# Attention and experts on one core: the output projection tile by tile in the next chunk, and the value product in 64x64 pieces skewed over two units

## The chip, the cores and the metric

The kernel runs on one NeuronCore of a Trainium2 chip. The time is the device time of one execution in microseconds, the median of three runs. TensorE (PE in the rows) multiplies, VectorE (DVE), ScalarE (ACT) and GpSimd (POOL) work on elements, and SyncE (SP) issues DMAs. Each engine works through its own list in order; semaphores hold an instruction back until another engine has counted far enough.

## The reference

A transformer layer on 2x2048 tokens of 256 numbers: attention in a window of 128 keys over 16 heads of 64, and a mixture of 8 experts, top 2, with 640 slots per expert and choice.

```python
h = _layernorm(x) * (1 + ca) + sa
q, k, v = split(h @ Wqkv)                      # 16 heads of 64
scores = (q @ k.T) * scale                     # keys j with i-127 <= j <= i
attn = softmax(where(mask, scores, -max)) @ v
x = x + ga * (attn @ Wout)
h = _layernorm(x) * (1 + cb) + sb
probs = softmax(h @ gate_w.T + gate_b); topk_prob, topk_idx = top_k(probs, 2)
# each token goes to a slot of its two experts, in order of tokens, at most 640 per expert and choice
y = sum over choices of prob * (relu(xb @ W1 + b1) @ W2 + b2)
x = x + gb * y
```

## The kernel before

**Tiling.** The 4096 tokens are 8 chunks of 512 (`NC`), a chunk is 4 tiles of 128. The projections and the output use pairs of 16-bit numbers (high and low part, three products each); scores, transposes and the value product work on 32-bit numbers. A chunk has 16 *units*: a pair of heads `j` and one half (`part`) of the chunk, that is 4 tiles of 128 queries by 256 keys.

**Steps.** A chunk runs in 16 steps, `i` = 4 to 19 (`STEPS`). In step `i` TensorE makes the scores of unit `i` (from 16 on those of the next chunk's first four), the value product of unit `i-4`, the transposes of unit `i-2` and one projection of q or k for the next chunk, in steps 12, 13, 14 and 16 also one tile of the first half of the next chunk's values. VectorE masks, takes the row maxima, normalises the unit before, and at every second step forms the low part of the attention output; ScalarE does the exponentials of unit `i-1` (`exponentials`), the high part (`attn_high`), the copy of the turned probabilities out of PSUM (`copy_probT`) and the copies of the projections; GpSimd splits the turned probabilities into the part for the block before and the part for the own block (`split_keys`), zeroing what the mask forbids.

**Between chunks.** After step 19 TensorE makes the second half of the next chunk's values (`projections_after`, 4 tiles) and the output projection of the whole chunk (`project_out`, 96 matmuls of 256 columns), and VectorE adds it to `x` (`add_attention`).

**Routing.** The tokens of the chunk before are normalised, scaled, packed and sent to the experts' slots along the steps: `ROUTE_AT` says at which step each part stands. GpSimd does the scale and shift, and the scattering DMAs (`scatter`). In the last chunk the steps are others (`LAST_AT`, `EARLY_AT`), and the last projections (`LATE`) are made there.

**PSUM.** Two banks each for the two score buffers, one for the transposes (`pt`), one for the value product (`pv`), and two (`gen`) that all projections, logits, counts and outputs take in turn: `group_order` gives the n-th group bank n mod 2, and a group waits until the engine that empties the one before it in this bank has done so (`claim`). All orders are written out by hand; nothing is scheduled by a program.

The lines that the change touches most:

```python
for hd in range(2):                                  # L666, value product, two matmuls of 256 columns
    mm = pe.matmul(pv[r:r + DH, 2 * part * P:(2 * part + 2) * P], v[:, 2 * part + 1, h * DH:(h + 1) * DH], ...)
for i in range(2):                                   # L671, four of 128
    for hd in range(2):
        mm = pe.matmul(pv[r:r + DH, b * P:(b + 1) * P], v[:, b + i, h * DH:(h + 1) * DH], ...)
```

## Time and profile before

| | us |
|---|---|
| three timed runs, median (lowest, highest) | 1151.61 (1149.98, 1154.63) |
| profiled execution, its own time | 1147.24 |
| its span | 1144.4 |
| chunk 0, steps and what follows (54.4 to 135.4) | 81.0, TensorE busy 79.7 |
| chunk 1 (135.4 to 218.7) | 83.3, TensorE busy 81.6 |
| chunk 6 (551.8 to 625.6) | 73.8, TensorE busy 68.9 |
| last chunk and way into the experts (625.6 to 760) | 134.4, TensorE busy 110.6 |
| experts (760 to the end) | 384.4, TensorE busy 373.0 |

Over the span TensorE is busy 95%, VectorE 66%, ScalarE 58%, GpSimd 44%. The granted clock of TensorE is full (1.00) in all attention chunks but the last (0.95). A time in a row is counted from the start of the span. The last column of a timeline row, in brackets, is the idle time of the engine ahead of the row and what ended it.

### The profile page before, as it was taken

To read this page: it belongs to the slowest core of one execution; us is meant where nothing else is said; L and a number is where in the kernel's file an instruction comes from. 1 tells how busy PE (TensorE), PEld (TensorE's weight loads), DVE (VectorE), ACT (ScalarE), POOL (GpSimd) and SP (SyncE) were. 2 spreads that over 40 slices of the span, in tenths; PEclk is the share of its full clock that TensorE was granted. 3 is DMA by queue.
4 is the path that set the end of the run, shared out by engine and by line. 5 is a ranking of instruction groups with operands and counts; after the bars stand their busy time and mean duration, and the time that the engine had idled before them with its cause. 6 is when DMAs were issued, how large, how long until landed. Compare 5 with 4: busy or idle time off the path is not lost.

```text
span 1144.4 us, 25293 instructions
## 1 busy us (share of the span) xinstructions
PE 1084.4 (95%) x9469; PEld 711.8 (62%) x9469; DVE 750.3 (66%) x1663; ACT 660.5 (58%) x1874; POOL 506.2 (44%) x555
## 2 busy tenths in 40 slices
PE   7999999999999999999998885989999999999996
PEld 4455655655655655655656564756776858585765
DVE  5776586586576585674675784756676766666653
ACT  5677476476476476476473853447474563727461
POOL 2234274365275365355445655434344352525342
PEclk9999999999999999999999998999999999999998
DMA  9744111112021021021031024434345353534000
GB/s 335 151 163 138 40 29 48 38 37 52 27 45 48 24 46 45 24 45 39 24 103 48 5 83 121 92 94 81 109 94 153 97 112 111 112 112 78 23 20 9
DMA packets 140114, 87.41 MB, mean 76 GB/s; under 512 B 96708, under 2 KB 130650, under 8 KB 139868
## 3 DMA queue, kind: packets, MB, share of 16 engines
q1 hardware_dynamic: 129244, 64.29, 21.4%
q0 software_dynamic: 10752, 21.54, 6.6%
q8 instruction: 75, 1.23, 0.5%
q14 instruction: 43, 0.35, 0.1%
HBM read 40.02 MB, written 33.79 MB: 64 GB/s over the span
## 4 chain that ended last, share of the span: by engine, by line
PE 75%; issue 7%; DVE 7%; ACT 6%; POOL 4%; DMA 0%; SPq 0%; POOLq 0%; DVEq 0%; ACTq 0%
PE down L1617 18%; PE up L1603 17%; PE gen L600 10%; PE gen L614 7%; PE gen L691 6%; PE score L637 4%; PE pv L668 4%; PE pt L648 4%; ACT prob L909 4%; PE pv L675 3%; DVE prob L1121 2%; POOL h L370 1%; POOL probT_split L1424 1%; PE gen L699 1%; POOL probT_split L1422 1%
## 5 line engine op out<-in xcount | busy, mean ns | idle before, releaser
L1643 ACT ACTIVATE hid<-up,b1T 128x512 f16<-128x512 f32 (+2 forms) x192 | 124.3, 648 | 182.1 <-PE up L1603 180.3
L1603 PE MATMUL up<-xT,w 128*128 128x512 f16 (+2 forms) x1152 | 212.5, 346 | 10.9 <-issue 10.9
L1617 PE MATMUL down<-w,hid 128*128 128x256 f16 x1920 | 213.7, 274 | 3.2 <-DVE hid L1659 3.2
L1422 POOL TENSOR_SCALAR_AFFINE_SELECT probT_split<-probT 128x512 f32<-128x512 f32 x128 | 102.9, 804 | 250.9 <-ACT probT L917 247.4
L1617 PEld LDWEIGHTS down<-w,hid 128*128 128x128 f16 x1920 | 188.6, 98 | 27.6 <-DVE hid L1659 3.7
L600 PE MATMUL gen<-hT,big 128*128 128x512 f16 x768 | 185.0, 380 | 0.6 <-DVE hT L1371 0.6
L909 ACT ACTIVATE prob<-score,negmax 128x128 f32<-128x128 f32 x512 | 180.7, 375 | 0.7 <-DVE negmax L1113 0.7
L1603 PEld LDWEIGHTS up<-xT,w 128*128 128x128 f16 x1152 | 112.9, 98 | 104.9 <-issue 12.8
...
L1659 DVE TENSOR_TENSOR hid<-hid 128x512 f16<-128x512 f32 (+2 forms) x192 | 115.2, 606 | 72.4 <-ACT hid L1644 72.0
L917 ACT ACTIVATE probT<-pt 128x512 f32<-128x512 f32 x128 | 76.9, 601 | 99.0 <-PE pt L648 98.8
L1109 DVE COPY_PREDICATED score<-above,score 128x512 f32<-128x512 int32 x112 | 77.5, 692 | 77.3 <-PE score L637 77.2
L1644 ACT ACTIVATE hid<-up,b1T 128x512 f32<-128x512 f32 (+2 forms) x192 | 124.8, 650 | 0.0
L600 PEld LDWEIGHTS gen<-hT,big 128*128 128x128 f16 x768 | 73.8, 98 | 67.7 <-issue 1.2
L637 PE MATMUL score<-k,q 64*64 64x192 f32 (+2 forms) x2048 | 111.0, 330 | 2.6 <-issue 2.2
L909 ACT ACTIVATION_READ_ACCUMULATOR prob<-score,negmax 128x1 f32 x512 | 111.0, 217 | 0.0
...
L1121 DVE TENSOR_TENSOR prob<-prob,rinv 128x512 f32<-128x512 f32 x128 | 103.4, 808 | 0.0
L668 PE MATMUL pv<-probT_split,v 128*64 128x256 f32 x512 | 83.5, 403 | 19.0 <-DVE attn L1134 7.0
L637 PEld LDWEIGHTS score<-k,q 64*64 64x64 f32 x2048 | 64.5, 132 | 53.9 <-issue 51.6
L614 PE MATMUL gen<-big,hT 128*128 128x512 f16 x384 | 89.1, 379 | 2.3 <-DVE logit L1160 1.2
L1424 POOL TENSOR_SCALAR_AFFINE_SELECT probT_split<-probT 128x512 f32<-128x512 f32 x128 | 86.3, 674 | 0.0
...
## 6 DMA issues: line engine op xcount, KB each, us to landing
...
kept<-out,tail POOLq DMA_INDIRECT x80, 3.1
out<-y,tail POOLq DMA_INDIRECT x80, 2.4
...
```

Source lines behind the costliest of these rows:

```text
L600: mm = pe.matmul(dst[:], wqkv[:, kd, a, col:col + P], hT[:, cn % 2, kd, b, :], start=(n == 0), stop=(n == 5))
L614: mm = pe.matmul(dst[:], hT[:, cn % 2, kd, a, s * P:(s + 1) * P], wqkv[:, kd, b, 2 * INNER + half * 512:2 * INNER + (half + 1) * 512], sta ...
L637: mm = pe.matmul(dst[lo:lo + HALF, 2 * hd + i, first:lo + P + HALF], q[r:r + DH, j, b * P + lo:b * P + lo + HALF], k[r:r + DH, j, b * P + ...
L668: mm = pe.matmul(pv[r:r + DH, 2 * part * P:(2 * part + 2) * P], v[:, 2 * part + 1, h * DH:(h + 1) * DH], probT_split[:, par, 2 * hd:2 * hd ...
L909: mm = act.activation(prob[:, h % 2, b, :], score[h % 2][:, b, P:], ACT.Exp, bias=negmax[:, h % 2, b:b + 1], accum_out=rowsum[:, h % 2, b: ...
L1121: dve.tensor_tensor(prob[:, h % 2], prob[:, h % 2], rinv[:, h % 2, :].unsqueeze(2).to_broadcast([P, TILES, P]), ALU.mult)\
L1422: pool.affine_select(out=probT_split[:, h % 2, :, 1], in_=probT[:, h % 2], pattern=[[0, TILES], [1, P]], compare_op=ALU.is_ge, fill=zero, ...
L1603: mm = pe.matmul(bank, w1[:, par, kd, a, ft * P:(ft + 1) * P], part_rows(e, n, xT[:, par, b * KD + kd, :]), start=(i == 0), stop=(i == 5))
L1617: mm = pe.matmul(down[n][:, s, :], hid[:, ft, a, t * P:(t + 1) * P], w2[:, par, ft, b, :], start=(i == 0), stop=(i == 3 * FT - 1))
L1643: act.activation(part_rows(e, n, hid[:, ft, 0, :]), bank, ACT.Relu, scale=1 / W_SCALE, bias=bias).then_inc(hid_hi, 1)
L1644: act.activation(part_bank(e, n, hid32[:, k_ % 4, :]), bank, ACT.Relu, scale=1 / W_SCALE, bias=bias).then_inc(up_out, 1)
L1659: dve.tensor_tensor(part_rows(e, n, hid[:, ft, 1, :]), part_bank(e, n, hid32[:, k_ % 4, :]), part_rows(e, n, hid[:, ft, 0, :]), ALU.subtra ...
```

## The change

- The output projection of chunk c is made tile by tile in steps 4, 6, 8 and 11 of chunk c+1 (`OUT_TILE`, `late_out`, `add_tile`), and the second half of the values of a chunk in its own steps 5, 7, 9 and 10 (`SECOND_V`). Chunk 6 makes its output at its own end as before, in pairs of tiles (`project_out_pair`).
- The value product of chunks 0 to 6 is cut into 64x64 pieces: `high_keys` takes keys 64 to 127 of a block, `low_keys` keys 0 to 63; pieces that the mask empties are left out. In step `i` the high keys of unit `i-4` stand in turn with the low keys of unit `i-5` (`half_values`), also over the border of two chunks. There are two banks `pv` now, one per parity of the unit.
- The transposes take the two `gen` banks like everything else (`("pt", i)`); their own bank is gone. ScalarE copies them straight to `probT_split`, which is a ring of three, and GpSimd splits in place.
- Routing is spread over two chunks: rows in steps 8 to 16 (`ROUTE_AT`), logits to scatter in steps 4 to 13 of the next (`CHOOSE_AT`); for round 6 they stand at the end of chunk 6.
- The high and low parts of the attention output are made per unit (256 columns) in a ring of 24 slots (`attn_slot`). `x` holds 6 chunks instead of 8 (`X_PLACE`), the last two are loaded late. The weights of expert 0 are loaded after chunk 6's rows are stored.

```diff
+X_PLACE = (2, 3, 0, 1, 4, 5, 2, 3)
+X_CHUNKS = max(X_PLACE) + 1
+ATTN_SLOTS = H + PAIRS
+LATE_PACKED = (ATTN_SLOTS - H) * 4 * P
 EARLY_TILES = 3
+RING = 3
...
 score = [ps(f"score{i}", [P, TILES, 2 * P], F32) for i in range(2)]
-pt = ps("pt", [P, TILES, P], F32)
-pv = ps("pv", [P, CHUNK], F32)
+pv = [ps(f"pv{i}", [P, CHUNK], F32) for i in range(2)]
 gen = [ps(f"gen{i}", [P, 512], F32) for i in range(2)]
...
+OUT_TILE = {4: 0, 6: 1, 8: 2, 11: 3}
+SECOND_V = {5: 0, 7: 1, 9: 2, 10: 3}
+ROUTE_AT = {"stats": (8, 13), "rstd": 13, "norm": 14, "scale": 14, "shift": 15, "token": 16, "pack": 16, "low": 16}
+CHOOSE_AT = {"logits": 4, "softmax": 5, "exp": 5, "top": 6, "counts": 7, "slots": 8, "send": 9, "sent": 13}
...
+        names += [("pt", i)]
+        if c > 1:
+            names += ([("logits",)] if i == CHOOSE_AT["logits"] else []) + ([("counts",)] if i == CHOOSE_AT["counts"] else [])
         if c > 0:
...
+            names += [("tile", OUT_TILE[i])] if i in OUT_TILE else []
+            names += [("own v", SECOND_V[i])] if i in SECOND_V else []
+        names += projections_at(c, i)
...
+        def high_keys(c, u, hd, i, cur):
+            n_unit = H * c + u
+            j, part = unit_of(c, u)
+            r, h, b = DH * hd, 2 * j + hd, 2 * part + i
+            first = HALF * cur
+            return pe.matmul(pv[n_unit % 2][r:r + DH, i * P + first:(i + 1) * P], v[HALF:, b + cur, h * DH:(h + 1) * DH],
+                             probT_split[HALF:, n_unit % RING, 2 * hd + i, cur, first:], start=(i == 0 and cur == 0),
+                             stop=False, skip_group_check=True)
+        def low_keys(c, u, hd, i, cur):
+            n_unit = H * c + u
+            j, part = unit_of(c, u)
+            r, h, b = DH * hd, 2 * j + hd, 2 * part + i
+            last = P if cur else HALF
+            return pe.matmul(pv[n_unit % 2][r:r + DH, i * P:i * P + last], v[0:HALF, b + cur, h * DH:(h + 1) * DH],
+                             probT_split[0:HALF, n_unit % RING, 2 * hd + i, cur, 0:last], start=False,
+                             stop=(cur == 0), skip_group_check=True)
+        def half_values(c, new, old):
+            if old is not None:
+                pe.wait_ge(high_done, H * old[0] + old[1] + 1)
+            if new is not None:
+                values_there(c, new)
+            for i in range(2):
+                for n in range(2):
+                    for hd in range(2):
+                        if new is not None:
+                            high = high_keys(c, new, hd, i, n)
+                        if old is not None:
+                            low = low_keys(*old, 1 - hd, i, 1 - n)
+            if new is not None:
+                high.then_inc(high_done, 1)
+            if old is not None:
+                low.then_inc(pv_done, 1)
...
+        def late_out(c, t):
+            if c == 0 and t == 0:
+                pe.wait_ge(split_lo, 8)
+            pe.wait_ge(attn_lo, H * c + (H - 1 if t < 2 else H))
+            dst, full = claim(c + 1, ("tile", t))
+            project_out_tile(c, dst[:, 0:D], t, range(PAIRS)).then_inc(full, 1)
...
+                if c == LAST - 1 and i == STEPS[-1]:
+                    half_values(c, i - HI_AT, (c, i - LO_AT))
                     scores(c, i)
-                weighted_values(c, i - 4)
...
+                    half_values(c, None, (c, H - 1))
+                else:
+                    scores(c, i)
+                    half_values(c, i - HI_AT, (c, i - LO_AT) if i >= LO_AT else (c - 1, H - 1) if c > 0 else None)
+                transposes(H * c + i - 2, c, ("pt", i))
+                if c > 1 and i == CHOOSE_AT["logits"]:
+                    route_logits(c - 1)
+                if c > 1 and i == CHOOSE_AT["counts"]:
+                    route_counts(c - 1)
+                if c > 0 and i in OUT_TILE:
+                    late_out(c - 1, OUT_TILE[i])
+                if c > 0 and i in SECOND_V:
+                    project_v(c - 1, 1, [SECOND_V[i]])
+                for name in projections_at(c, i):
+                    project(c, name)
+            if c == LAST - 1:
...
-            act.activation(probT[:, h % 2], pt[:], ACT.Copy).then_inc(probT_ready, 1)
...
+            bank, before = turned_in(u)
+            act.wait_ge(gen_full[bank], before + 1)
+            at_least(act, pv_done, u - RING + 1)
+            act.activation(probT_split[:, u % RING, :, 1], gen[bank][:].rearrange("p (a q) -> p a q", q=P), ACT.Copy)\
+               .then_inc(gen_free[bank], 1)
         def attn_high_part(c, u):
             j, part = unit_of(c, u)
...
             act.wait_ge(pv_done, H * c + u + 1)
...
+            if c > 0 and u == ATTN_SLOTS - H:
+                bank, before = group(c - 1, ("out", 1)) if c == LAST else group(c, ("tile", TILES - 1))
+                act.wait_ge(gen_full[bank], before + 1)
+            act.activation(attn[:, attn_slot(c, j, part), 0, :], pv[(H * c + u) % 2][:, 0:2 * P], ACT.Copy).then_inc(attn_hi, 1)
...
+                exponentials(c, i - 1)
+                if i >= LO_AT:
+                    attn_high_part(c, i - LO_AT)
+                elif c > 0:
+                    attn_high_part(c - 1, H - 1)
+                if c > 1 and i == CHOOSE_AT["exp"]:
+                    route_exp(c - 1)
+                if c > 0 and i == at["pack"]:
                     route_pack(c)
                 if i == LN_AT[1] + 1 and c + 2 < NC:
                     ln_pack(c + 2)
...
+                copy_probT(c, i - 2)
+                if c > 0 and i in SECOND_V:
+                    values(c - 1, ("v", 1, SECOND_V[i]))
+                for name in projections_at(c, i):
+                    evacuate(c, name)
+            if c == LAST - 1:
+                attn_high_part(c, H - 1)
                 for name in projections_after(c):
                     evacuate(c, name)
...
+                route_exp(c)
...
+        def add_tile(c, t):
+            bank, before = group(c + 1, ("tile", t))
+            if c == 0 and t == 0:
+                dve.wait_ge(mod_spread, 16)
+            at_least(dve, x2_ready, TILES * c + t)
+            dve.wait_ge(gen_full[bank], before + 1)
+            dve.scalar_tensor_tensor(gated[:, t % 2, :], gen[bank][:, 0:D], 1 / W_SCALE, modrow[:, batch(c), 0, :],
+                                     ALU.mult, ALU.mult).then_inc(gen_free[bank], 1)
+            dve.wait_ge(gen_free[bank], before + 1)
+            row = x[:, x_at(c) + t, :]
+            dve.tensor_tensor(row, row, gated[:, t % 2, :], ALU.add).then_inc(x2_ready, 1)
...
+                if i > LO_AT:
+                    attn_low_part(c, i - LO_AT - 1)
+                elif c > 0:
+                    attn_low_part(c - 1, H + i - LO_AT - 1)
+                if c > 0 and i == LO_AT:
+                    keep_v(c - 1, 1)
+                if c > 0 and i - 1 in OUT_TILE:
+                    add_tile(c - 1, OUT_TILE[i - 1])
+                if c > 1 and i == CHOOSE_AT["softmax"]:
+                    route_softmax(c - 1)
+                if c > 1 and i == CHOOSE_AT["slots"]:
+                    route_slots(c - 1)
+                if c == 0 and i % 2 == 0:
+                    keep_first_keys((i - LAG) // 2)
+                if i == 13:
+                    keep_v(c, 0)
+                softmax_step(c, i, False)
+                if c > 0 and i in at["stats"]:
+                    half = at["stats"].index(i)
+                    dve.wait_ge(x2_ready, TILES * (c - 1) + 2 * half + 2)
+                    norm_stats(dve, x_at(c - 1), stats[1], meanvar[1], r_stat, r_mv, stats_before(c) + half + 1,
+                               range(2 * half, 2 * half + 2))
+                if c > 0 and i == at["norm"]:
+                    norm_rows(dve, x_at(c - 1), h2, meanvar[1], rstd[1], r_rstd, r_xn, c)
+                if c > 0 and i == at["token"]:
+                    route_tokens(c)
+                if c > 1 and i == CHOOSE_AT["top"]:
+                    route_top(c - 1)
+                if i in LN_AT and c + 2 < NC:
+                    ln_shift(c + 2, LN_AT.index(i))
+                if i == LN_NEXT and c + 3 < NC:
+                    ln_first(c + 3)
+                if i == LN_NEXT + 1 and c + 3 < NC:
+                    ln_second(c + 3)
+            if c == LAST - 1:
+                for u in range(H - 2, H):
+                    attn_low_part(c, u)
+                keep_v(c, 1)
+                route_softmax(c)
+                route_top(c)
+                add_attention(c, 0)
+                route_slots(c)
+                add_attention(c, 1)
...
-            pool.affine_select(out=probT_split[:, h % 2, :, 1], in_=probT[:, h % 2], pattern=[[0, TILES], [1, P]],
+            bank, before = turned_in(u)
+            pool.wait_ge(gen_free[bank], before + 1)
+            whole, own = probT_split[:, u % RING, :, 1], probT_split[:, u % RING, :, 0]
+            pool.affine_select(out=own, in_=whole, pattern=[[0, TILES], [-1, P]],
+                               compare_op=ALU.is_gt, fill=zero, base=0, channel_multiplier=1).then_inc(prev_ready, 1)
+            pool.affine_select(out=whole, in_=whole, pattern=[[0, TILES], [1, P]],
                                compare_op=ALU.is_ge, fill=zero, base=0, channel_multiplier=-1).then_inc(cur_ready, 1)
-            pool.affine_select(out=probT_split[:, h % 2, :, 0], in_=probT[:, h % 2], pattern=[[0, TILES], [-1, P]],
...
+                if c > 1 and pick["send"] <= i < pick["send"] + TILES:
+                    scatter(c - 1, [i - pick["send"]])
+                if c > 1 and i == pick["sent"]:
+                    pool.wait_ge(sent, 16 * TILES * K * (c - 1))
+                if i == LN_NEXT + 1 and c + 3 < NC:
+                    ln_rstd_of(c + 3)
+            if c == 0:
+                pool.wait_ge(zero_sent, 16 * (SLOTS // P))
+            if c == LAST - 1:
+                scatter(c, range(TILES))
+                pool.wait_ge(sent, 16 * TILES * K * c)
```

**TensorE in a step with nothing but scores, values, transposes and a projection, before** (L637 scores, L668 and L675 value product, L648 transposes, L600 a projection of k; `pv` and `gen` are PSUM banks):

```order
L637 MATMUL score1<-k,q 64x192 x8
L668 MATMUL pv<-probT_split,v 64x256 x2
L675 MATMUL pv<-probT_split,v 64x128 x4
L648 MATMUL pt<-identf,prob 128x128 x4
L600 MATMUL gen1<-hT,big 128x512 x6
```

**The same engine after, first step of chunk 3** (L716 high keys of the new unit, L725 low keys of the old one; L686 scores, L696 transposes; below the first half of the pieces, the second is the same again):

```order
L686 MATMUL score0<-k,q 64x192 x8
L716 MATMUL pv0<-probT_split,v 64x128
L725 MATMUL pv1<-probT_split,v 64x128
L716 MATMUL pv0<-probT_split,v 64x128
L725 MATMUL pv1<-probT_split,v 64x128
L716 MATMUL pv0<-probT_split,v 64x64
L725 MATMUL pv1<-probT_split,v 64x64
L716 MATMUL pv0<-probT_split,v 64x64
L725 MATMUL pv1<-probT_split,v 64x64
...
L696 MATMUL gen0<-identf,prob 128x128 x4
L826 MATMUL gen1<-gate16,h2T 128x8 x24
L768 MATMUL gen0<-wout,attn 128x256 x24
```

The six value matmuls of one unit have become sixteen, eight of them of the unit before, in the other bank. The logits (L826) and output tile 0 (L768) stand behind the transposes, and tile 0 takes the bank that the transposes have just filled.

**TensorE between two chunks before** (L614 values, second half; L691 output projection):

```order
L600 MATMUL gen1<-hT,big 128x512 x6
L614 MATMUL gen0<-big,hT 128x512 x6
L614 MATMUL gen1<-big,hT 128x512 x6
L614 MATMUL gen0<-big,hT 128x512 x6
L614 MATMUL gen1<-big,hT 128x512 x6
L691 MATMUL gen0<-wout,attn 128x256 x48
L691 MATMUL gen1<-wout,attn 128x256 x48
L637 MATMUL score0<-k,q 64x192 x8
```

This block is gone but for chunk 6; its parts stand as the tiles of L768 and L663 in the steps of the next chunk.

**VectorE ahead of step 5 of a chunk, after** (L1368 low part, L1211 the values' last tile kept for the next chunk, L1264 and L1268 addition of output tile 0, L1282 the logits read out of PSUM, L1222 the mask of step 5):

```order
L1234 TENSOR_TENSOR prob<-prob,rinv 128x512
L1368 TENSOR_TENSOR attn<-pv1,attn 128x256
L1211 COPY v<-v 128x512
L1264 SCALAR_TENSOR_TENSOR gated<-gen0,modrow 128x256
L1268 TENSOR_TENSOR x<-x,gated 128x256
L1282 SCALAR_TENSOR_TENSOR logit<-gen1,gbB 128x32
L1222 COPY_PREDICATED score1<-above,score1 128x4x128
```

The addition and the logits were at the chunk's end and in step 13; now the reading of the logits, which empties gen1, stands behind the addition of tile 0. The low part follows each normalisation (L1234) instead of every second.

**ScalarE in step 16, after** (L1045 packing of the routed rows, L1024 copy of the turned probabilities, L998 q, L1005 values):

```order
L1015 ACTIVATE prob,rowsum<-score1,negmax 128x128 x4
L1033 ACTIVATE attn<-pv1 128x256
L1045 ACTIVATE packed<-h2 128x4x256
L1024 ACTIVATE probT_split<-gen0 128x4x128
L998 ACTIVATE q<-gen1 128x512
L1005 ACTIVATE v<-gen0 128x512
```

The packing was in step 9, two steps behind the shift; it is now one step behind it, ahead of the copy that empties gen0 for the value tile.

## Rows read from the trace of the kernel before

**Rows 1.** Busy time by stretch, chunk 3; columns as in the first row.
```profile
core 0: us, PE busy (x) PEld busy (x) DVE busy (x) ACT busy (x) POOL busy (x), PEclk, DMA share, GB/s
...
302.10:385.20 83.10, 81.44 (x795) 50.04 (x794) 56.37 (x139) 51.36 (x179) 41.79 (x48) 1.00 0.15 40
```

**Rows 2.** Timeline of TensorE, one step of chunk 3: start, duration, line, tiles, count.
```profile
305.77 0.88 PE L637 MATMUL score<-k,q 64*64 64x192 f32 x16
306.58 0.65 PE L668 MATMUL pv<-probT_split,v 128*64 128x256 f32 x4
307.06 0.61 PE L675 MATMUL pv<-probT_split,v 128*64 128x128 f32 x8
307.60 0.66 PE L648 MATMUL pt<-identf,prob 128*128 128x128 f32 x4
308.10 1.46 PE L600 MATMUL gen<-hT,big 128*128 128x512 f16 x6
309.49 0.88 PE L637 MATMUL score<-k,q 64*64 64x192 f32 x16
```

**Rows 3.** Timeline of TensorE, between chunks 3 and 4.
```profile
369.40 5.34 PE L614 MATMUL gen<-big,hT 128*128 128x512 f16 x24
374.58 10.64 PE L691 MATMUL gen<-wout,attn 128*128 128x256 f16 x96
```

**Rows 4.** Timeline of TensorE, chunk 3, steps 8 and 12.
```profile
316.91 0.88 PE L637 MATMUL score<-k,q 64*64 64x192 f32 x16
318.38 0.65 PE L668 MATMUL pv<-probT_split,v 128*64 128x256 f32 x4 [0.59 <-POOL probT_split L1424]
...
335.24 0.75 PE L740 MATMUL gen<-gate,h2T 128*128 128x8 f16 x24
...
337.51 1.47 PE L614 MATMUL gen<-big,hT 128*128 128x512 f16 x6 [0.21 <-DVE logit L1160]
```

**Rows 5.** Timeline of TensorE, windows of 0.1 and 0.7 us at two scores.
```profile
302.06 0.39 PE L637 MATMUL score<-k,q 64*64 64x192 f32 x4
...
353.56 0.77 PE L637 MATMUL score<-k,q 64*64 64x64 f32 x16
354.27 0.44 PE L668 MATMUL pv<-probT_split,v 128*64 128x256 f32 x2
```

**Rows 6.** Timeline of ScalarE, the step of rows 2.
```profile
306.37 0.36 ACT L909 ACTIVATE prob<-score,negmax 128x128 f32<-128x128 f32 x1
...
307.74 0.62 ACT L923 ACTIVATE attn<-pv 128x512 f16<-128x512 f32 x1
308.30 0.60 ACT L917 ACTIVATE probT<-pt 128x512 f32<-128x512 f32 x1
```

**Rows 7.** Timeline of VectorE, the step of rows 2, and step 10.
```profile
308.57 0.68 DVE L1121 TENSOR_TENSOR prob<-prob,rinv 128x512 f32<-128x512 f32 x1
309.17 0.69 DVE L1134 TENSOR_TENSOR attn<-pv,attn 128x512 f16<-128x512 f32 x1
...
328.09 1.11 DVE L1121 TENSOR_TENSOR prob<-prob,rinv 128x512 f32<-128x512 f32 x1
```

**Rows 8.** Timeline of GpSimd, chunk 3.
```profile
314.35 2.36 POOL L370 TENSOR_TENSOR h<-h,modrow 128x1024 f32<-128x1024 f32 x1 [4.01 <-DVE h L237]
...
328.03 0.63 POOL L1424 TENSOR_SCALAR_AFFINE_SELECT probT_split<-probT 128x512 f32<-128x512 f32 x1
```

**Rows 9.** Timeline of TensorE, chunk 6, step 14 and after step 19.
```profile
593.06 0.88 PE L637 MATMUL score<-k,q 64*64 64x192 f32 x16
...
612.38 2.75 PE L614 MATMUL gen<-big,hT 128*128 128x512 f16 x12
```

**Rows 10.** Timeline of GpSimd, scattering DMAs at the end of chunk 6.
```profile
602.59 1.11 POOL L1433 DMA_INDIRECT slot_inputs<-packed,send  x1 [1.98 <-DVE send L1227]
604.00 0.98 POOL L1433 DMA_INDIRECT slot_inputs<-packed,send  x1 [0.30 <-PE pv L675]
...
618.73 0.63 POOL L1422 TENSOR_SCALAR_AFFINE_SELECT probT_split<-probT 128x512 f32<-128x512 f32 x1 [1.61 <-DMA slot_inputs<-packed,send]
```

**Rows 11.** Timeline of SyncE's queue, the four transposes for chunk 2.
```profile
111.80 6.17 SPq L535 DMA_TRANSPOSE hT<-h  x4
```

561 lines of the change are left out of this document (268 added, 293 removed).

## Prediction

> **What bounds the kernel now.** I read the busy time by stage first: the table above and, for one full chunk, [rows 1]. One full round of the attention (a chunk of 512 tokens, 16 head units) takes 83.1 us of which TensorE is busy 81.4, at the full granted clock; VectorE is busy 56, ScalarE 51, GpSimd 42. So a chunk costs what TensorE has to do plus its few waits. By the table chunk 0 takes 81.0, chunks 1 to 5 83.3 each, chunk 6 73.8, the last chunk and the way into the experts 134, the experts 384. The change touches the first 626 us and the last chunk.
>
> The timeline of TensorE in a step without extras [rows 2] gives scores 306.58-305.77 = 0.81, value product 307.60-306.58 = 1.02, transposes 0.50, one q or k projection 1.39: 3.72 us, and the next step follows at once. Between two chunks stand 24 matmuls of values (5.2 us) and 96 of the output projection (10.6 us) [rows 3]: TensorE is busy all through, so there is no hole to fill there. TensorE's waits inside a chunk are small. Taking each step's scores-to-values distance against 0.81, and the 0.36 before a value projection, they are 0.66, 0.25, 0.26, 0.36 and 0.57, together 2.1 us; the first and the fourth are in [rows 4], on GpSimd's split of the turned probabilities and on VectorE's logits. The others are on the split and on VectorE's low half of the attention output.
>
> **The value product.** Before, a unit has 2 matmuls of 256 columns and 4 of 128; each column half of the array gets 256+2x128 = 512 columns. Now each quarter of the array gets 2x128+2x64 = 384, because 64x64 blocks that the mask empties are left out, and the upper keys of one unit run beside the lower keys of the unit before. What a column costs follows from [rows 2]: scores put 2x192 = 384 columns through the busiest quarter in 0.81, values 512 in 1.02. Two equations: 1.64 ns a column and 0.18 us fixed for going from one kind of product to the next. The first unit of a batch checks it: 128+192 = 320 columns in the busiest quarter, 0.18+0.52 = 0.70, measured 354.27-353.56 = 0.71 [rows 5].
>
> Now scores and values are both of the 64x64 kind, so I count the fixed part once: 0.18+768x1.64 = 1.44 against 0.81+1.02 = 1.83. That is a gain of 0.39 at most; the pieces per quarter rise from 4 to 8, for which I keep back 0.03 and take **0.36 us a step**. The low bound is the fixed part paid twice: 0.36-0.18 = 0.18. Both are estimates from [rows 2, 5]. Chunks 0 to 6 have 112 such steps. In the last six of chunk 6 TensorE doesn't set the pace (below): 106x0.36 = **-38.2 us**.
>
> How close small matmuls can follow: 24 of 8 columns over the whole array take 0.61 us, 25 ns each [rows 4], while four passes of scores, each in another quarter, cover 0.39 us together [rows 5]; one after another, at 192x0.82 ns each, they would cover over 0.63. The Trainium skill (TensorE: Matmul & The Clock Gate, "Wait — 56ns, not 53.3ns?") says that start-to-start never drops below about 25 ns however small a matmul is. By it the 32 passes of a unit's values would need 0.80 us instead of 0.63. The logits agree; the scores' row speaks against such a floor across quarters, and no run here shows 32 in a row. The same skill (TensorEngine Tiling (Array Packing), "Key Properties") says that changing the tiling mode drains the array; the 0.18 fixed agrees in kind, and by that rule it is paid once.
>
> **Output projection and second half of the values.** The same 96+24 matmuls, moved into steps 4 to 11 of the next chunk: 0 us of work. Chunk 6 keeps its own output at its end. On VectorE two additions of 512 columns (0.69 each op) become four of 256; the low half of the attention goes from 8x512 to 16x256, and it is now wanted in every step. VectorE has 27 us of slack a chunk, so only the places count. The old waits go with the old places: 2.1 in each of chunks 1 to 5 and about 1.5 in chunk 6: **-12.0 us**.
>
> **What is late next.** The transposes lose their own bank and share the two gen banks, in turn. Times below are from a step's start. A copy of the turned probabilities now ends at about 2.95: exponentials run 0.59 to 1.97, the high half of 256 columns takes some 0.35 (an estimate from 0.56 for 512), the copy 0.6 [rows 6].
>
> a) Step 4, chunks 2 to 6: transposes gen0, logits gen1, tile 0 gen0, q0 gen1. Tile 0 is reached at 2.58 and waits for the copy, 0.4. It ends at 5.6. VectorE stands at the addition of tile 0, and the logits behind it are what frees gen1 for q0: about 0.2 to hear of it, two additions of 0.35, 0.18 for the logits: 6.8 instead of 5.6. Together 1.6.
> b) Step 7, chunks 2 to 6: counts take gen1, so the value tile needs gen0 at 2.3 and waits until 2.95; k1 then meets VectorE's route_slots within 0.1. Together 0.75.
> c) Steps 10 and 11: normalising rows of 0.88 to 1.6 delay the low half, which TensorE wants 0.70 into a step: 0.2.
> d) Steps 15 and 16: GpSimd has scale and shift of 2.36 each [rows 8] two steps apart, fed by VectorE's 1.6 us of rows at step 14. Scale ends 2.85 into step 15, so the split behind it reaches TensorE 0.25 late; VectorE's low half adds 0.2. Shift ends 3.25 into step 16; ScalarE's packing (1.05) stands in step 16 ahead of the copy, which ends at 5.0 instead of 2.95, and the value tile in gen0 was due at 3.66: 1.35. Together 1.8.
> e) Step 18: statistics and rows of chunk c+3 (1.8+1.7) now lie in steps 16 and 17: 0.5.
>
> Sum 4.85 a chunk in chunks 2 to 5: 19.4. Chunk 1 has only c to e, 2.5, and one thing more: the 80 zero rows hold SP until 111.8, then four transposes end at 118.0 plus their landing [rows 11]; chunk 0 now ends near 113.4 and q0 wants them at 118.0: 1.5. Chunk 6, first ten steps: 2.5. **+25.9 us.** The bounds of this term are wide: some of these waits lie under each other, 0 at the lowest; twice as much if VectorE's extras meet GpSimd's (its normalise takes 0.68 alone and 1.11 when a split has begun before it [rows 7, 8]).
>
> Chunk 6, steps 14 to 19, have no q and k. Before they took 612.38-593.06 = 19.3 for 14 us of work [rows 9]. Now scale, shift and low stand in exactly these steps: 5.2 until the rows are there, scale, split, shift, split, packing, low, two splits, 2.36+1.4+2.36+1.4+0.1+2.4+3x1.45: about 20.6 with the value tile (1.3) that moved in. **0 us.**
>
> Into the last chunk: round 6's scatter, 8 DMAs, is now one block after its slots. Logits come 3.4 after step 19, the first output pair at 8.7, two additions and the slots at 12.2. The pairs of DMAs cost 1.11+0.30+0.98 [rows 10], so 9.5 for eight, and 1.6 for the landing [rows 10]: 23.3. TensorE is there at 14.1+5.8+0.8 = 20.7 and needs one split, 0.8 to 1.5, more: 3.5 to 4. The last chunk has waits on GpSimd of its own later and takes part of it back: **+2.5 us.** The weights of expert 0 load later, but 7.8 us ahead of their use in step 7.
>
> **Sum**: -38.2-12.0+25.9+0+2.5 = -21.8 us. The profiled execution took 1147.2 (span 1144.4), so 1125.4; the median of the three timed runs lies 4.4 above it. Forecast 1129, a little under 1129.8.
>
> **Rivals.**
> R1, the small pieces cost more: the fixed part is paid twice (0.18), or each of the 32 passes holds TensorE for 25 ns as the logits' matmuls do, 32x0.025 = 0.80 instead of 384x1.64 = 0.63 (0.17). 106x0.17 = 18 us of the gain are gone: 1147. For it: every other change of product in [rows 2] costs this; against: between the two kinds of value matmuls nothing extra stands. The floor named by TensorE: Matmul & The Clock Gate in the Trainium skill would act in this way.
> R2, slower than before: VectorE's low half decides each step. The place is TensorE's value product at step i, which wants the low half of unit i-6; VectorE does that one right after normalising [rows 7]. Normalise starts 2.8 into a step, ends at 3.4, low half 0.4 more: 3.85, wanted at 3.36+0.70 = 4.06. The margin is 0.2. If the copy of the turned probabilities is ready before 2.8, GpSimd's split goes first and normalise takes 1.11: TensorE then waits about 0.45 in all 106 steps, +48 us: 1177. It decides from a delay of 0.2 on; by my count the split begins at 2.98, 0.17 after normalise (starts of both from [rows 6, 7], less the shorter high half).
> R3, the waits a to e mostly cover each other, half of 25.9: 1116.
>
> **Numbers.** Forecast 0.60, R1 0.20, R2 0.10, R3 0.10. A difference under 0.5% (5.8 us) can't be told from none. Faster by more: forecast, R3, and somewhat under half of R1, 0.78; within 0.5%: the rest of R1, 0.11; slower 0.11. Range 1112 (under R3) to 1151 (over R1); the 0.10 of R2 stays out.
>
> **What would show it.** Quiet steps of TensorE of 3.36 instead of 3.72, and scores to transposes 1.47 instead of 1.83 (R1: 1.65). Chunks 2 to 5 at 80.4, chunk 0 at 59. Waits of q0 on VectorE's logits in step 4, of tile 0 and step 7's and step 16's value tile on ScalarE's copy. A wait of TensorE on VectorE's low half in nearly every step would be R2. In chunk 6 the last six steps unchanged near 20, and one wait on GpSimd of 3 to 4 us at the second unit of the last chunk. I am wrong if a full chunk still takes over 83.

## The result, and the profile after

The changed kernel takes 1157.61 us (median of 7 runs, 1155.87 to 1160.58) where the kernel before takes 1151.61 (7 runs, 1149.69 to 1154.63): 1.0053 times as long, 95% interval 1.0038 to 1.0068. Forecast were 1129, and 1151 as the upper end of the range. The profiled execution took 1158.6, its span 1155.9.

The experiments ran in five groups. Kernels of one group ran one after the other on one chip, with runs of the kernel before among them (medians 1151.8, 1149.4, 1150.6, 1153.4, 1148.0). In three further measurements the changed kernel took 1.0048 (1.0035 to 1.0062), 1.0067 (1.0040 to 1.0093) and 0.9991 (0.9975 to 1.0006) of it: it is a little slower, or the same, and never the 2% faster that was forecast.

What was promised of the value product is there. A quiet step of the changed kernel (chunk 3, against [rows 2]; the columns are start, busy us, engine, line, operation):

```profile
325.39 0.88 PE L686 MATMUL score<-k,q 64*64 64x192 f32 x16
326.09 0.27 PE L725 MATMUL pv<-probT_split,v 64*64 64x128 f32 x1
...
326.87 0.66 PE L696 MATMUL gen<-identf,prob 128*128 128x128 f32 x4
327.36 1.46 PE L649 MATMUL gen<-hT,big 128*128 128x512 f16 x6
328.75 0.88 PE L686 MATMUL score<-k,q 64*64 64x192 f32 x16
```

328.75-325.39 = 3.36 us instead of 3.72, and 326.87-325.39 = 1.48 from scores to transposes (forecast 1.47). But TensorE is no longer busy all through. The first block shows one full chunk (chunk 4) and the last chunk, with the columns of [rows 1]; the second what TensorE waits for up to the last chunk (what ends the wait, then us in total, times, longest):

```profile
363.90:446.50 82.60, 77.75 (x1111) 51.93 (x1110) 58.38 (x156) 51.77 (x187) 43.88 (x49) 1.00 0.16 40
...
621.50:714.90 93.40, 64.85 (x677) 42.41 (x676) 59.60 (x164) 45.39 (x148) 51.11 (x58) 0.93 0.27 81
```

```profile
PE pv L716 <- DVE attn L1368: 8.5, 9, 2.2
PE gen L663 <- ACT probT_split L1024: 7.5, 12, 0.9
PE gen L649 <- DVE logit L1282: 6.2, 5, 1.2
PE pv L716 <- POOL probT_split L1565: 5.8, 8, 1.7
PE gen L696 <- issue: 1.8, 7, 0.3
PE gen L768 <- issue: 1.2, 4, 0.3
```

A full chunk still takes 82.6, of which TensorE is busy 77.8; in [rows 1] it was 81.4 of 83.1. The busy time went down by 3.7 and the idle time up by 3.2. (In the profile without pauses, of which more below, chunk 4 takes 80.5, with 76.5 busy.) Here is where each profiled execution left the forecast's sum (1125.4 us of execution, 1122.6 of span). The column of the forecast is the time of before with the terms of its own sum (for a full chunk they give 80.3; its text says 80.4); the second profile is that of the fifth group.

| stretch, us | before | forecast | after, first profile | after, fifth group |
|---|---|---|---|---|
| up to chunk 0 | 54.4 | 54.4 | 55.0 | 55.8 |
| chunk 0 | 81.0 | 59.4 | 62.3 | 62.3 |
| chunk 1 | 83.3 | 79.4 | 77.5 | 77.5 |
| chunks 2, 3, 4, 5 | 83.3, 83.1, 83.4, 83.3 | 80.3 each | 82.7, 86.5, 82.7, 82.5 | 80.8, 83.6, 80.5, 79.8 |
| chunk 6 | 73.8 | 87.0 | 92.4 | 90.6 |
| last chunk to the first expert product | 81.8 | 84.3 | 93.4 | 100.0 |
| from there to the end | 437.0 | 437.0 | 441.0 | 437.7 |

The first profile is 33.2 us over the sum. Of these 11.5 are pauses in chunks 2 to 6 that came in some groups and not in others (the two profiles' chunks differ by that), 9.1 the last chunk, and 8.1 what both profiles share in chunks 0 to 6: chunks 0, 3 and 6 are 2.9, 3.3 and 3.6 over, chunk 1 is 1.9 under. The 4.0 us in the experts are in the first profile alone (the other three of this kernel give 437.7 to 438.5); their cause stays open. In the fifth group's profile the last chunk alone is 15.7 over.

### The profile page after: what moved, and what is told of

Read it like the earlier page. It is cut to its first block, busy times and chain, and to the rows that moved or that the text cites. A ratio compares the mean times of both kernels' runs of the same rounds, so it can differ in the third digit from the quotient of the medians.

```text
span 1155.9 us, 29944 instructions
## 1 busy us (share of the span) xinstructions
PE 1065.9 (92%) x11709; PEld 728.6 (63%) x11709; DVE 764.2 (66%) x1743; ACT 664.2 (57%) x1930; POOL 516.0 (45%) x555
## 4 chain that ended last, share of the span: by engine, by line
PE 75%; DVE 7%; ACT 6%; issue 6%; POOL 4%; DMA 1%; SPq 0%; DVEq 0%; ACTq 0%; another core or an unknown queue 0%; POOLq 0%
PE down L1773 17%; PE up L1759 17%; PE gen L649 12%; PE gen L768 7%; PE gen L663 6%; PE score L686 5%; PE gen L696 4%; ACT prob L1015 3%; PE pv L725 3%; PE pv L716 2%; DVE prob L1234 1%; POOL h L404 1%; POOL h L408 1%; ACT probT_split L1024 1%; DVE xn L1185 1%
## 5 line engine op out<-in xcount | busy, mean ns | idle before, releaser
L1563 POOL TENSOR_SCALAR_AFFINE_SELECT probT_split<-probT_split 128x512 f32<-128x512 f32 x128 | 110.2, 861 | 260.4 <-ACT probT_split L1024 255.7
L649 PE MATMUL gen<-hT,big 128*128 128x512 f16 x768 | 187.8, 384 | 11.5 <-DVE logit L1282 6.2
L1858 POOL DMA_INDIRECT out<-y,tail x80 | 82.5, 1031 | 209.9 <-DVE y L1843 195.9
L1222 DVE COPY_PREDICATED score<-above,score 128x512 f32<-128x512 int32 x112 | 77.7, 694 | 98.9 <-PE score L686 98.6
L686 PE MATMUL score<-k,q 64*64 64x192 f32 (+2 forms) x2048 | 111.0, 330 | 2.2 <-issue 2.2
L716 PE MATMUL pv<-probT_split,v 64*64 64x64 f32 (+1 forms) x1792 | 97.0, 245 | 14.6 <-DVE attn L1368 8.5
L716 PEld LDWEIGHTS pv<-probT_split,v 64*64 64x64 f32 x1792 | 92.4, 133 | 25.0 <-issue 23.9
L663 PE MATMUL gen<-big,hT 128*128 128x512 f16 x384 | 92.6, 380 | 9.1 <-ACT probT_split L1024 7.5
L725 PE MATMUL pv<-probT_split,v 64*64 64x128 f32 (+1 forms) x1792 | 99.9, 246 | 0.2
L686 PEld LDWEIGHTS score<-k,q 64*64 64x64 f32 x2048 | 64.5, 132 | 55.4 <-issue 52.7
L725 PEld LDWEIGHTS pv<-probT_split,v 64*64 64x64 f32 x1792 | 93.8, 133 | 1.8 <-issue 0.2
```

Of the source, the lines that this page charges most:

```text
L649: mm = pe.matmul(dst[:], wqkv[:, kd, a, col:col + P], hT[:, cn % 2, kd, b, :], start=(n == 0), stop=(n == 5))
L663: mm = pe.matmul(dst[:], hT[:, cn % 2, kd, a, s * P:(s + 1) * P], wqkv[:, kd, b, 2 * INNER + half * 512:2 * INNER + (half + 1) * 512], sta ...
L686: mm = pe.matmul(dst[lo:lo + HALF, 2 * hd + i, first:lo + P + HALF], q[r:r + DH, j, b * P + lo:b * P + lo + HALF], k[r:r + DH, j, b * P + ...
L716: return pe.matmul(pv[n_unit % 2][r:r + DH, i * P + first:(i + 1) * P], v[HALF:, b + cur, h * DH:(h + 1) * DH], probT_split[HALF:, n_unit ...
L725: return pe.matmul(pv[n_unit % 2][r:r + DH, i * P:i * P + last], v[0:HALF, b + cur, h * DH:(h + 1) * DH], probT_split[0:HALF, n_unit % RIN ...
L1563: pool.affine_select(out=own, in_=whole, pattern=[[0, TILES], [-1, P]], compare_op=ALU.is_gt, fill=zero, base=0, channel_multiplier=1).the ...
```

## The experiments

**The value product, undone.** Chunks 0 to 6 use the old product in the new arrangement:

```diff
-    half_values(c, i - HI_AT, (c, i - LO_AT) if i >= LO_AT else (c - 1, H - 1) if c > 0 else None)
+    weighted_values(c, i - HI_AT)
```

> The changed kernel with one part undone: chunks 0 to 6 use the value product of before (2 matmuls of 256 columns and 4 of 128 per unit, all keys of one unit together) in the new arrangement of output projection, values and routing. Forecast's term: 0.36 us in each of 106 steps where TensorE sets the pace, 38 us: 1196. If steps that wait for VectorE, ScalarE or GpSimd hide part of it, the chunks 2 to 5 lose less than 5.8 us each: with four or five waiting steps a chunk, 4.0 to 4.8, and about 1185 to 1190.

Measured: 1172.47 (first group). The chunks 0 to 6 take 578.3 together against 555.0 for the changed kernel in its profile without pauses (the fifth group's): the new product is worth 23.3 us there, not 38.2. Step by step the difference is 0.35 where TensorE sets the pace. But step 16 is 5.49 with the old and 6.19 with the new product, step 18 4.20 and 4.37: there TensorE waits for something that stands at its own time, and shorter steps before only make the wait longer. Another 1.3 is step 17 of chunk 3 (7.23 and 8.54), where TensorE's granted clock fell in the one profile and not in the other; more on it below. It was run again beside the changed kernel:

> The old value product in the new arrangement once more, against the changed kernel on the same chip. Worth of the new product by the step lengths of the two profiles so far: 0.35 in each quiet step, less where a step waits for something else; 3.4 to 4 a chunk, about 24 to 27 in all: the time is that much above the changed kernel's. If TensorE's pauses come from its many instructions (32 small matmuls a unit instead of 6, 40% more instructions in all), this kernel has none on the chip that shows them, and the difference is only 15 to 18 there.

> The changed kernel once more, as the partner on one chip of the three that follow. So far one chip showed TensorE pausing with nothing to wait for while the scatter's packets are out (steps 9 to 13 of chunks 2 to 6, 2 us a chunk), another chip did not, in other variants. If it is the chip: either this run has the pauses and the three others have them too where they issue as many TensorE instructions, or none has. 1153 to 1158 with them, 1145 to 1149 without.

Measured in the third group: 1172.16 against 1156.93, so the new product was worth only 15.2 there. The reason is in the next rows.

**The pauses.** In the first profile, in steps 9 to 13 of chunks 2 to 6, TensorE stops between two instructions with nothing to wait for that the profile shows; its granted clock is 1.00 there. Step 10 of chunk 3, first profile:

```profile
314.67 0.33 PE L696 MATMUL gen<-identf,prob 128*128 128x128 f32 x1
315.17 0.42 PE L696 MATMUL gen<-identf,prob 128*128 128x128 f32 x2 [0.17 <-issue]
315.91 0.27 PE L696 MATMUL gen<-identf,prob 128*128 128x128 f32 x1 [0.32 <-issue]
316.01 1.46 PE L663 MATMUL gen<-big,hT 128*128 128x512 f16 x6
```

and the same step of the same program in the fifth group:

```profile
313.43 0.66 PE L696 MATMUL gen<-identf,prob 128*128 128x128 f32 x4
313.92 1.46 PE L663 MATMUL gen<-big,hT 128*128 128x512 f16 x6
```

Four transposes cover 1.51 us instead of 0.66. GpSimd issues the scatter's DMAs in steps 9 to 12; outside steps 9 to 13 no step of these chunks differs between the two profiles by more than 0.2. Steps 9 to 13 of chunk 3 take 26.1 instead of 23.5.

> The changed kernel itself, run once more beside the others. In its first profile VectorE's first instruction of a step (the mask of the new scores) starts 0.3 to 0.8 us after everything it needs, in the four steps 9 to 12 of chunks 2 to 6 in which GpSimd issues the scatter's DMAs, and steps 9 to 13 together take 24.5 to 26.2 us; in the three variants of it run so far it starts after 0.07, and these steps take 23.5. Theory 1 (the stalls belong to this program, whatever chip runs it): they are back, chunks 2 to 5 take 82.5 and more, and the time is 1155 to 1160. Theory 2 (they belonged to that one placement on a chip): chunks 2 to 5 at 80.8, the experts at 437 instead of 441, and 1142 to 1148.

Measured: 1154.42, and the pauses were back in all four kernels of this second group (the changed kernel's chunks 2 to 5 took 82.5, 84.2, 82.5, 81.7). The three variants of the first group had none. In the third group the changed kernel, `spread_again` and `best1` had them, and `whole_again`, with 6 matmuls a unit instead of 32, had not: its steps 9 to 13 take 25.1 in both groups. So the scatter alone doesn't make them; this one comparison speaks for the many small instructions as a second condition (TensorE and its loads issue 10955 instructions from 200 to 600 us, in the kernel before 7855). I then put the old product into these steps only:

```diff
+    elif c > 1 and 9 <= i <= 14:
+        scores(c, i)
+        if i == 9:
+            half_values(c, None, (c, i - LO_AT))
+        if i < 14:
+            weighted_values(c, i - HI_AT)
+        else:
+            half_values(c, i - HI_AT, None)
```

> The changed kernel with the old value product (6 matmuls a unit instead of 32) in steps 9 to 13 of chunks 2 to 6 only, where the scatter's DMAs go out, and the new one elsewhere; at step 9 TensorE does the low keys of the unit before apart, at step 14 the high keys alone. Instruction theory (TensorE pauses there because its instructions are too many for what it is fed while the scatter's packets are out): VectorE's mask follows the scores after 0.07 in all these steps; by lengths they take 5 x 0.35 more work but 2.0 to 2.6 less of pauses, so the time is within 3 us of the changed kernel's. Rival (the pauses come from the scatter alone): they stay, and the time is 8 us longer, 1163 to 1165.

Measured: 1155.46, in the fourth group, in which no kernel paused; so it tells nothing of the pauses. (Step 9 takes 5.67 instead of 4.66, since the low keys of one unit stand alone.)

> The changed kernel a fourth time. Three chips were met in the calls so far: on one, every kernel with the new value product paused in the scatter's steps, on two, none did, and the four edits together took 1137.3 on the first and 1125.8 on another. If that holds for the change alone, it takes 1154 to 1157 where its profile shows the pauses (chunks 2 to 5 at 82 to 85) and 1143 to 1148 where it does not (chunk 2 at 80.8), which would be below the kernel before.

Measured: 1147.39, the kernel before 1147.96. This was the same chip as in the second and third group, and there was no pause. The time that the expectation gave for a run without pauses (1143 to 1148) holds, but its reason, the chip, does not: neither the chip nor the program decides alone, and within a group all went the same way. What it is stays open. The Trainium skill (Runtime: NRT & Kernel Launch, "Instruction fetch mechanics") says that an engine's instructions are fetched in blocks of 16 KiB, 256 instructions each, by a DMA queue of their own. The trace agrees on the size (42 fetches, 672 KB, for these 10955 instructions), but not on a cause: the fetches next to the pause above begin at 309.4 and 320.5.

**The last chunk: block of scatter DMAs and weights of expert 0.** The change puts the eight DMAs of round 6 in one block ahead of the last chunk's second split, and behind them asks for 2 MB of weights. The weights moved back into chunk 6 (they go to other places in the memory for that, the old ones being still in use, and ScalarE's splits of them get one more wait):

```diff
-store_rows(LAST - 1)
 sp.wait_ge(kept_clean, 1)
 sp.wait_ge(x2_sent, 16 * (LAST - 1))
+sp.wait_ge(r_xn, LAST - 1)
 load_expert(sp, weights_32(0), 0)
+store_rows(LAST - 1)
```

> The changed kernel with one thing moved back: the 2 MB of expert 0's weights are asked for near the end of chunk 6's steps, ahead of the store of chunk 6's rows, into the places of x that chunks 4 and 5 have left, and no longer at the start of the last chunk. Theory (collision): in the changed kernel this transfer fills the DMA engines just when ScalarE, TensorE and GpSimd enter the last chunk's code; the second step of that chunk takes 11.9 us instead of 5.8, ScalarE's first high half there starts 4.5 us after its data, and the landing of the scatter takes 4.7 us instead of 1.6. With the transfer gone from there the second step should be 7 to 9 us, and the whole 4 to 8 us shorter: 1150 to 1154. Rival (the block of eight scatter DMAs on GpSimd alone makes the step long): the step stays at 10 us or more and the time within 2 us of 1157.6.

Measured: 1141.85, 0.9927 (0.9898 to 0.9956) of the kernel before. The 15.8 us to the first measurement are not all this edit's, since its group had no pauses. Against the fifth group, without pauses too but on another chip, it is 5.5 in the medians and 9.2 in the last chunk of the profiles (90.8 for 100.0). TensorE and GpSimd at the second unit of the last chunk, with the weights early:

```profile
617.97 0.97 POOL L1575 DMA_INDIRECT slot_inputs<-packed,send  x1 [0.30 <-issue]
...
620.57 0.63 POOL L1564 TENSOR_SCALAR_AFFINE_SELECT probT_split<-probT_split 128x512 f32<-128x512 f32 x1 [1.62 <-DMA slot_inputs<-packed,send]
...
621.88 1.12 PE L755 MATMUL pv<-probT_split,v 128*64 128x256 f32 x4 [4.00 <-POOL probT_split L1564]
```

and in the changed kernel (fifth group), with TensorE's granted clock of this stretch (the column behind GpSimd's, then the DMA share and GB/s):

```profile
618.19 0.97 POOL L1574 DMA_INDIRECT slot_inputs<-packed,send  x1 [0.30 <-issue]
...
624.07 0.63 POOL L1563 TENSOR_SCALAR_AFFINE_SELECT probT_split<-probT_split 128x512 f32<-128x512 f32 x1 [4.91 <-DMA slot_inputs<-packed,send]
...
625.39 1.12 PE L754 MATMUL pv<-probT_split,v 128*64 128x256 f32 x4 [7.82 <-POOL probT_split L1563]
...
628.21 4.12 PE L649 MATMUL gen<-hT,big 128*128 128x512 f16 x12
```

```profile
616.00:622.00 6.00, 0.88 (x16) 0.56 (x16) 2.52 (x9) 1.99 (x9) 2.56 (x3) 0.89 1.00 347
622.00:628.00 6.00, 2.60 (x16) 1.98 (x17) 0.18 (x1) 0.38 (x1) 3.65 (x6) 0.50 0.23 85
628.00:634.00 6.00, 5.27 (x32) 2.29 (x33) 1.90 (x5) 2.83 (x10) 3.60 (x3) 0.75 0.00 0
```

With the weights early the scatter lands after 1.62, as in [rows 10], and TensorE waits 4.00: the forecast's 3.5 to 4. With the weights behind it the landing takes 4.91, because the DMA engines are full (share 1.00, 347 GB/s), and TensorE waits 7.82. Its granted clock falls from 2.4 to 1.2 GHz during the wait in both kernels, and it stays low for longer behind the longer one: here it is 0.50 from 622 to 630 us (in the middle row above) and 1.00 again from 632; with the weights early it is 0.50 for some 3 us:

```profile
621.80:624.00 2.20, 2.12 (x13) 1.50 (x14) 0.00 (x0) 0.10 (x1) 2.12 (x4) 0.50 0.00 0
```

So q and k take 4.12 here and 2.81 with the weights early, and this step 16.4 and 11.2, instead of 5.8. The expectation had 7 to 9, the rival 10 or more with nothing gained in time: both were half right. In the groups with pauses the loss lies in two steps (11.9 and 6.9 in the first profile). The two steps together are 18.8 to 22.2 in all nine profiles with late weights and a block, 17.1 with early weights and a block, 11.6 in that of before. To see whether the transfer harms by itself, the kernel before got it at the same place (`load_expert` behind the last `store`, splits in steps 7 to 10):

> The kernel before with the same transfer moved the other way: expert 0's weights are asked for at the start of the last chunk instead of during chunk 6, and their splits stand two steps later (steps 7 to 10), as in the changed kernel. The scatter, the value product and all the rest are those of before. Collision theory: the first steps of the last chunk grow by 3 to 6 us and the time is 1154 to 1158. Rival (the transfer is harmless, the scatter block is what costs): within 2 us of 1151.6.

Measured: 1153.21, 1.0018 (0.9998 to 1.0038), and its first steps stay at 5.81. In these two kernels the transfer harms only where somebody waits for another DMA while it is under way. The other way, the weights late and the scatter spread:

```diff
-scatter(c, range(TILES))
-pool.wait_ge(sent, 16 * TILES * K * c)
...
+if i == 7:
+    pool.wait_ge(sent, 16 * TILES * K * (c - 1))
 split_keys(c, i - 3)
+for n in {4: (0, 1, 2), 5: (3, 4, 5), 6: (6, 7)}.get(i, ()):
+    scatter(c - 1, [n // K], [n % K])
```

> The changed kernel with round 6's eight scatter DMAs no longer in one block ahead of the last chunk's second split but three, three and two behind the splits of its steps 4, 5 and 6, with the wait for their landing ahead of step 7's split. The transfer of expert 0's weights stays where the change put it. Theory of the forecast (the block is what TensorE waits for at the second unit): that wait goes, 4 us or more. Collision theory: ScalarE's high half still starts late (it hangs on nothing of GpSimd), so the second step keeps most of its 11.9 us, and what is won is 1 to 3 us; the landing may now be waited for in step 7.

Measured: 1136.19, 0.9871 (0.9846 to 0.9895), and all three steps at 5.81. In the third group, with the pauses, 1148.19 (0.9981), 8.7 less than the changed kernel beside it (the expectation said 9 to 12). By the two steps' lengths the block costs 5.5 alone (17.1 against 11.6) and the late weights some 5 on top of it (22.2 in the fifth group); without the block they cost nothing.

> The spread scatter once more, now against the changed kernel on the same chip. Block theory (TensorE waits for the split behind the block: 4.0 us, plus 5 where the weights' transfer delays the landing): 9 to 12 us less than the run before it, whichever chip. If the earlier 21 us belonged to this edit alone, 20.

**Two exchanges.** Term a of the forecast, on VectorE in step 5, `route_softmax` ahead of `add_tile` instead of behind it:

> The changed kernel with one exchange on VectorE: in step 5 of chunks 2 to 6 the logits are taken out of their bank ahead of the two additions of the first output tile, not behind them. The forecast priced that wait of TensorE (term a) at 1.2 us a chunk; the profile shows step 4 at 8.45 us for 6.6 us of work. Theory: step 4 falls to about 7.2 and the time by 5 to 6 us. Rival: the tile's own bank then comes free later and step 6 or the next projection waits instead; under 2 us.

Measured: 1150.88, 3.5 less than the changed kernel of its group (expected: 5 to 6). The wait is the one forecast (1.2). First the changed kernel, then the exchange:

```profile
283.83 0.42 DVE L1268 TENSOR_TENSOR x<-x,gated 128x256 f32<-128x256 f32 x1
284.18 0.18 DVE L1282 SCALAR_TENSOR_TENSOR logit<-gen,gbB 128x32 f32<-128x32 f32 x1
...
284.50 1.46 PE L649 MATMUL gen<-hT,big 128*128 128x512 f16 x6 [1.25 <-DVE logit L1282]
```

```profile
280.27 0.18 DVE L1282 SCALAR_TENSOR_TENSOR logit<-gen,gbB 128x32 f32<-128x32 f32 x1
...
281.84 1.46 PE L649 MATMUL gen<-hT,big 128*128 128x512 f16 x6
282.11 0.42 DVE L1264 SCALAR_TENSOR_TENSOR gated<-gen,modrow 128x256 f32<-128x256 f32 x1 [1.14 <-PE gen L768]
```

Step 4 falls from 8.45 to 7.04 to 7.14 in five chunks, 7 us in the profile (span 7.7 shorter); the medians of the timed runs show half of that. The second exchange, on ScalarE in step 16, `route_pack` behind `copy_probT`:

> The changed kernel with one exchange on ScalarE: in step 16 of chunks 1 to 6 the packing of the routed rows (1.05 us) stands behind the copy of the turned probabilities and not ahead of it. Step 16 takes 6.2 us for 4.66 of work. Theory: it falls to 4.7 to 5.1 in chunks 1 to 5, 6 us in all. Rival: GpSimd's shift, not the packing, sets the copy's follower, and the wait comes back in step 17: under 2 us.

Measured: 1153.13, 1.3 less than its partner: under 2, as the rival had it. The changed kernel, step 16 of chunk 2:

```profile
262.06 1.06 ACT L1045 ACTIVATE packed<-h 128x1024 f16<-128x1024 f32 x1 [0.74 <-POOL h L408]
263.02 0.58 ACT L1024 ACTIVATE probT_split<-gen 128x512 f32<-128x512 f32 x1
...
263.66 1.47 PE L663 MATMUL gen<-big,hT 128*128 128x512 f16 x6 [0.92 <-ACT probT_split L1024]
```

The exchange takes step 16 from 6.20 to 5.09, but step 17 grows from 4.66 to 5.31 and step 18 shrinks from 4.36 to 3.36: 1.5 a chunk. In chunk 3 it gives 4 back: step 17 there goes from 7.1 to 11.0, of which only 1.1 is a longer wait (3.25 for 2.16); the rest, 2.9, is TensorE's clock, as shown below.

**Step 17 of chunk 3.** The changed kernel, first profile:

```profile
343.10 2.36 POOL L408 TENSOR_TENSOR h<-h,modrow 128x1024 f32<-128x1024 f32 x1
343.12 2.63 DVE L1219 COPY_PREDICATED score<-above,no_prev 128x256 f32<-128x256 int32 x1 [0.15 <-PE score L686]
...
346.79 2.54 POOL L413 TENSOR_TENSOR packed<-h,packed 128x1024 f16<-128x1024 f32 x1
347.32 2.04 DVE L1273 CAST packed<-token_no 128x4 int32<-128x4 f32 x1
...
349.26 1.39 DVE L233 BATCH_NORM_STATS2 stats<-x 128x6 f32<-128x256 f32 x4
...
350.99 0.39 DVE L1368 TENSOR_TENSOR attn<-pv,attn 128x256 f16<-128x256 f32 x1
...
351.52 0.29 PE L716 MATMUL pv<-probT_split,v 64*64 64x128 f32 x1 [2.16 <-DVE attn L1368]
```

A copy of four numbers a row takes 2.04 us and a mask of 256 columns 2.63 (0.42 where GpSimd does nothing long): the copy ends with GpSimd's operation, the mask 0.3 after it. Behind them the low half comes late. What follows this wait differs from profile to profile, for the same program too. The q projection behind it, in the first profile and with the spread scatter, both after a wait of 2.16:

```profile
352.92 2.77 PE L649 MATMUL gen<-hT,big 128*128 128x512 f16 x6
...
348.53 1.46 PE L649 MATMUL gen<-hT,big 128*128 128x512 f16 x6
```

In the first the granted clock is 0.50 for some 3 us, in the second 1.00 throughout. Step 17 takes 7.05 where the clock stays and 8.5 to 8.7 where it falls; behind the wait of 3.25 it takes 8.14 where it stays and 9.8 to 11.0 where it falls. No run here shows what decides it.

Three more kernels: four edits together (weights early, scatter spread, both exchanges), the same without the early weights, and the four with the token numbers in step 18 (`"token": 16` becomes 18):

> All four at once in the changed kernel: weights of expert 0 asked for in chunk 6, scatter of round 6 spread over three steps, logits ahead of the additions, packing behind the copy. If the gains add up: 1136 (the spread scatter alone) less 5 for the logits and 6 for the packing, and 0 to 3 for the weights: 1122 to 1126. If they hide each other: 1130 or more.

> The four edits together once more, as the partner of the next two on one chip: 1137 on a chip where TensorE pauses in the scatter's steps, 1126 to 1130 on one where it does not.

> The same without the earlier load of expert 0's weights, that is with the transfer where the change put it. If the transfer's place still costs something once the scatter is spread: 2 to 5 us more than its partner. If it cost only by delaying the scatter's landing: within 1.5 us.

> The four edits, and VectorE writes the token numbers in step 18 instead of 16. In chunk 3 that copy of four numbers a row takes 2.04 us because it ends only when GpSimd's subtraction ends (elsewhere 0.60 behind a split). If TensorE's long step 17 of chunk 3 (7.1 to 11.0 us instead of 4.7) comes from it, 2 to 4 us less than the partner; if it comes from the masks of step 15 (2.6 us beside GpSimd's shift), nothing.

Measured: four edits 1137.29 in the second group (with pauses) and 1125.81 in the fourth (without); without the early weights 1124.43, so their place costs nothing once the scatter is spread; with all four and the token numbers in step 18 1122.59, 3.2 less than its partner. Step 17 of chunk 3 takes 6.20 there and its wait 1.31 instead of 3.25; the partner's step took 8.14 at the full clock, and 10.94 without the early weights, where the clock fell. In step 18 the copy takes 0.60:

```profile
347.30 0.60 DVE L1274 CAST packed<-token_no 128x4 int32<-128x4 f32 x1
```

This kernel is the best of all: 0.9733 (0.9694 to 0.9771) of the kernel before, and once more in the fifth group 1123.16, 0.9786 (0.9759 to 0.9812), 24 us under the changed kernel beside it.

> The four edits with the token numbers in step 18, once more beside the changed kernel: 1121 to 1125 on a chip without the pauses, 1131 to 1136 on one with them; 20 to 24 us less than the changed kernel in either case.

One attempt gained little: spread scatter, both exchanges, and the statistics and rows of chunk c+3 one step later (`LN_NEXT` 17).

> Changed kernel with the scatter of round 6 spread, the logits ahead of the additions, the packing behind the copy, and VectorE's statistics and rows of chunk c+3 one step later (17 and 18 instead of 16 and 17), where they no longer stand behind the token numbers that wait for GpSimd. Against the spread scatter alone: 1.3 x 5 for the logits, 2.3 x 5 less what returns in step 17 for the packing (net 1.4 x 5 by the step lengths of its profile), 2 for step 17 of chunk 3: 12 to 15 us less than it, 1122 to 1126. Rival: the statistics now collide with the next chunk's first low halves, and it is no better than 1130.

Measured: 1144.90, in the third group with its pauses, only 3.3 less than the spread scatter beside it. Steps 16 to 18 shrink, but step 19 takes 5.29 instead of 3.36 in chunks 0 to 2 and 4, 5.76 in chunk 3: the rival of that expectation.

## Why the prediction was wrong

- **Value product, -38.2.** The mechanism and the size per quiet step are right (3.36; R1 and R2 did not come). Wrong is the multiplication by 106: the product taken back is worth 23.3, since steps 16 and 18 and some of chunks 0 and 6 end with a wait that has its own time. The forecast had such waits in its other terms, so in the full chunks little is lost against it: without pauses chunks 2, 4 and 5 took 80.8, 80.5, 79.8, where its terms give 80.3.
- **Waits a to e, +25.9.** Together the two terms on waits came out: up to the last chunk TensorE's waits are 29.0 us in the profile without pauses and 15.0 in that of before, 14.0 more, and -12.0 with +25.9 makes 13.9. The parts came out less well, so some of this is luck. a is right (1.25 measured at q0); b was priced at 0.75, and the value tile of step 7 waits 0.45 (the rest of what that step takes over step 5 is the work of the counts); d was priced at 1.8 a chunk, and its largest part, step 16, is 1.54 over its work. Missing are new waits in chunk 0, which came out 2.9 over. The longest wait there, in step 10, is not new: it was 1.28 before and stands in the 81.0. New are 0.74 in step 13 and 0.41 in step 18 (rows below, the first from the kernel before); where the rest of the 2.9 comes from stays open. Missing is chunk 3, 3.3 over the forecast by the mutual blocking above and, for 1.5 of it, the fallen clock behind it; the forecast knew that normalising takes 0.68 or 1.11 beside GpSimd, and did not ask what the other operations of VectorE do there.

```profile
78.45 0.65 PE L668 MATMUL pv<-probT_split,v 128*64 128x256 f32 x4 [1.28 <-DVE attn L1134]
...
77.06 0.29 PE L716 MATMUL pv<-probT_split,v 64*64 64x128 f32 x1 [1.38 <-DVE attn L1368]
...
88.29 0.29 PE L716 MATMUL pv<-probT_split,v 64*64 64x128 f32 x1 [0.74 <-DVE attn L1368]
...
111.17 0.29 PE L716 MATMUL pv<-probT_split,v 64*64 64x128 f32 x1 [0.41 <-DVE attn L1368]
```

- **Chunk 6, 0.** Without pauses the chunk came out 3.6 longer than the sum. The last six steps took 21.4 instead of 19.3 where 20.6 was worked out (the parts named there give 19.6, and 20.9 with the value tile) and called nothing, and between the parts of its end stand the logits (0.7) and the counts with a wait (1.1), which the sum had left out. It left out as well that chunk 1 no longer has any logits and counts, which is most of the 1.9 that chunk 1 came out under it.
- **Into the last chunk, +2.5.** This is the step that failed most. The wait for the block was right (4.00 with the weights early, forecast 3.5 to 4), though the fallen clock behind it had no price. But the sentence "The weights of expert 0 load later, but 7.8 us ahead of their use" asked only when the weights are needed, and not what else is on the way: they delay the scatter's landing from 1.6 to 4.9 us, so the wait becomes 7.82, and the clock stays at half for some 10 us instead of 3. And the last chunk did not take "part of it back": even with the spread scatter it is 86.8 to the first expert product, 5 over before. So the stretch is 15.7 over the forecast in the profile without pauses and 9.1 in the first. One of its later waits is new, 2.16 us: the transposes stand in a `gen` bank that the addition of the first output pair still holds.

```profile
682.33 0.63 PE L696 MATMUL gen<-identf,prob 128*128 128x128 f32 x4 [2.16 <-DVE gated L1251]
```

- **What no term held**: the pauses, 11 us, in groups of runs that can't be told beforehand, with a cause that stays open. Without them the change is at 1147.4 against 1148.0, inside half a percent of no change, and still 18 above the forecast. The forecast's own test, "I am wrong if a full chunk still takes over 83", would have let the first profile pass (82.5 to 82.7 but for chunk 3); it should have named a bound nearer to its own 80.4, such as 81.5.
